# A two-layer mixer and expert kernel: three of the second scan's products dt\*x\*B move from VectorE to GpSimd

## The chip, the core and the metric

The kernel runs on one NeuronCore of a Trainium2 chip. Five engines work side by side and meet at semaphores: TensorE (PE in the profile; PEld is its weight load), VectorE (DVE), ScalarE (ACT), GpSimd (POOL) and SyncE (SP, which here only issues DMAs). Each engine runs its own instruction stream in order. Times are microseconds on the device, the whole kernel from start to end; the metric is the median of several executions.

## The reference, cut to what matters

The input x is [2, 128, 16, 16]: 2 batches of 256 tokens with 128 channels. Layer 0 is a selective state-space mixer (Mamba) followed by 8 experts (top 2), layer 1 a decaying sum over time followed by 16 experts (top 2). The part that the change touches is the mixer's scan, for 256 inner channels and 16 states:

```
dt = softplus(dt @ dt_proj_w.T + dt_proj_b);  A = -exp(A_log)
def step(h, inp):
    dt_t, B_t, C_t, x_t = inp
    dA = exp(dt_t[..., None] * A)
    h  = dA * h + (dt_t * x_t)[..., None] * B_t[:, None, :]
    y  = einsum('bdn,bn->bd', h, C_t)
y = scan(step); y = (y + xc * D) * silu(z); out = layernorm(clamp(y @ out_proj_w.T))
x = x + out;  x = x + experts(layernorm(x))      # layer 0, each token weighs 2 of 8 experts
```

## The kernel before, in words

Everything stays in SBUF. Channels lie on the 128 partitions; the 256 inner channels are two chunks (DC = 2), time (T = 256) is the free axis. The 16 states go in 8 pairs (PAIR = 2, NP = 8). With two batches that makes 16 pairs, numbered m = k + 8\*b; a tile of a pair holds 2 states x 2 chunks x 256 times = 1024 values in each partition. The work of pair m is:

- PE, `spread_b` (L990): transposes spread the two B rows over all partitions into the PSUM bank `b_ps` (one bank, one pair at a time).
- DVE, `inputs` (L695, instruction L702): the product dtx\*B into the PSUM tile `dbx[m % 2]`.
- ACT, `decays` (L508, L520): four exponentials make the decay factors in the SBUF tile `da[m % 4]`, up to four pairs ahead of the scan.
- DVE, `states` (L705, L712): one scan instruction along time, from `da` and `dbx` into the SBUF tile `hs[m % 2]`. It waits for `hc_done` of pair m-2, since `hs` has two buffers.
- POOL, `weigh` (L336, L343): the scan's states times the C rows, into `hc[m % 2]`. The C rows come by DMA from a small DRAM buffer, spread to all partitions, in three parts (`C_PARTS`).
- PE, `add` (L1000, L1004): matmuls with the identity sum the pair into PSUM.

All engines walk one list of steps, `plan` (L233 to L253), and each issues what it has in a step. For a pair the steps are `pair_in` and `pair_out`. DVE makes the product of pair m+1 in `pair_in` of pair m, and the scan of m in `pair_out`; POOL has nothing in `pair_in`, and `weigh` in `pair_out`. Between the pairs of the second batch (L241 to L247) the plan puts the tail of batch 0: its output projection, two norms, the routing and the first expert unit. The two lines that set this order are

```
before_states = {1: ["gate_out", "out_proj"], 3: ["inner_norm", "root_5"], 4: ["logits"], 5: ["softmax_e"], 7: ["lead"]}
after_states = {1: ["out_norm", "root_3"], 2: ["skip_norm", "skip_stats", "root_4"], 3: ["inner_scale", "to_channel"], ...}
```

The `root_` steps are inverse square roots on POOL (L310 to L313), for which DVE waits in the normalisation that follows: `skip_norm` needs `root_3`, `inner_norm` needs `root_4`. In steps `stage` (after `pair_in` of pairs k = 0 and 2) POOL makes the low parts of two expert weight blocks each (L357). `gates` and `softmax_e` (L785 to L813) route the tokens on DVE; the first `experts` unit needs the products of all 16 pairs done, since its PSUM banks are theirs, and the sum of pair 15 (`last_sum`) stands between units 1 and 2. After that PE works through 64 expert units (2 layers x 2 batches x 16).

Of the kernel before, what the change touches and what calls it, by code (L numbers as in the profile page):

```python
# [31 lines left out]
F32 = mybir.dt.float32  # L32
# [49 lines left out]
xt_ps var1 rstd1 var2 rstd2 xtok_ready taps_ps taps_ready wv_ps wv_ready xs_tok xs_ps xs_ready conv_ps xc_ready z_ps sz_ready  # L82
bct_ps bct_ready c_row_ready c_row_stored c0_loaded c1_loaded c2_loaded dt_ps abs_done r_done relu_done exp_dt ln_dt dt0_ready rounded dt1_ready dtx_ready
conv1_ps
# [8 lines left out]

def bass_metaformer(nc, x, packed, taps, rows, w1_0, w2_0, b2, decay, w1_1, w2_1, c_rows, out):
    with ExitStack() as ctx:
# [34 lines left out]
        b_tok = sb("b_tok", [128, NB, TT, NS])  # L130
        c_row = sb("c_row", [NS, NB, T])
        dt_a = per_batch("dt_a", [128, DC, T])
        dt_e = per_batch("dt_e", [128, DC, T])
        dt_l = per_batch("dt_l", [128, DC, T])
        dt_q = per_batch("dt_q", [128, DC, T])
# [87 lines left out]
        def between(work, end, groups, layer, b):  # L223
# [3 lines left out]
            for k in range(singles):  # L227
# [28 lines left out]
        @block.sync  # L256
        def _(sp):
            sp.dma_start(x_cm[:, 0, :], x[:, 0, :]).then_inc(s["x0_loaded"], 16)
            sp.dma_start(x_cm[:, 1, :], x[:, 1, :]).then_inc(s["x1_loaded"], 16)
            sp.dma_start(rows_sb[:], rows).then_inc(s["rows_loaded"], 16)  # L260
            sp.dma_start(par[:], packed).then_inc(s["params_loaded"], 16)
            sp.dma_start(cb[:, NP - DC:NP].rearrange("p c i t -> p (c i t)"), taps.to_broadcast([C, DC * TAPS * 128])).then_inc(s["taps_loaded"], 16)
            sp.dma_start(decay_sb[:], decay).then_inc(s["decay_loaded"], 16)
            sp.dma_start(b2_sb[:], b2).then_inc(s["b2_loaded"], 16)

            def weights(layer, i, w1_d, w2_d):
                n = EXPERTS[layer] // 2
# [9 lines left out]
            def c_rows_round(b):  # L277

                sp.wait_ge(s["c_row_ready"], b + 1)
                sp.dma_start(c_rows[b], c_row[:, b, :]).then_inc(s["c_row_stored"], 16)  # L280
                sp.wait_ge(s["c_row_stored"], 16 * (b + 1))
                for i, (k0, k1) in enumerate(C_PARTS):
                    if b:
                        sp.wait_ge(s["hc_done"], k1 + RING)
                    sp.dma_start(cb[:, k0:k1].rearrange("p k i t -> p (k i t)"),
                                 c_rows[b, PAIR * k0:PAIR * k1].rearrange("(o n) t -> o (n t)", o=1).to_broadcast([128, (k1 - k0) * PAIR * T])
                                 ).then_inc(s[f"c{i}_loaded"], 16)

            weights(0, 0, w1_0, w2_0)
            c_rows_round(0)  # L290
            weights(0, 1, w1_0, w2_0)
            for i in range(2):
                weights(1, i, w1_1, w2_1)
            c_rows_round(1)
# [7 lines left out]
        def _(pool):  # L302
# [88 lines left out]
            for step, *arg in plan:  # L391
# [7 lines left out]
                elif step == "root_5":  # L399
                    root_5(*arg)  # L400
                elif step == "step_1":
                    step_1()
                elif step == "step_x":
                    step_x()
                elif step == "stage":
                    low_part(0, arg[0], arg[0])
                elif step == "pair_out":
                    weigh(*arg, arg[1] % RING)
                elif step == "expert_in":
                    expert_in(*arg)  # L410
                elif step == "experts":
                    experts(*arg)
# [3 lines left out]
        def _(act):  # L416
# [91 lines left out]
            def decays(b, k, q):  # L508
# [3 lines left out]
                if b and k == 0:  # L512
                    act.wait_ge(s["dt1_ready"], 1)
                if m >= AHEAD:
                    act.wait_ge(s["h_done"], m + (1 + RING - AHEAD))
                for c in range(DC):
                    if b == 0 and k == 0:
                        act.wait_ge(s["dt0_ready"], c + 1)
                    for i in range(PAIR):
                        ins = nc.scalar.activation(da[q][:, i, c, 1:T], dt[:, c, b, 1:T], ACT.Exp,  # L520
                                                   scale=a_neg[:, c * NS + k * PAIR + i:c * NS + k * PAIR + i + 1])
# [73 lines left out]
        def _(dve):  # L595
# [99 lines left out]
            def inputs(b, k, p):  # L695
# [185 lines left out]
        def _(pe):  # L881
# [80 lines left out]
            def bc(b):  # L962
# [238 lines left out]
```

## Time and profile before

| | us |
|---|---|
| median of 3 runs | 215.6 (214.52 to 215.91) |
| the profiled execution | 212.92 |
| its span in the profile | 211.0 |
| busy in it: PE, PEld, DVE, ACT, POOL | 180.6, 149.6, 135.5, 120.1, 104.4 |

The span is the part of an execution that the profile shows. Lines such as L712 are lines of the kernel's file. A line of a timeline gives the start, the busy time, engine, line, operation, output and inputs, the shape, how many instructions are merged, and in brackets the idle time before it with what ended it. The instructions of one engine overlap by some 0.04 to 0.1 us, so the distance from start to start is what one of them costs in a queue.

### The profile page before, as it was taken

The numbers are of one execution on the slowest core, as the hardware profiler recorded it, in microseconds if no ns is written. First come the engines' busy times: TensorE is split into PE (matmuls) and PEld (weight loads), VectorE is DVE, ScalarE is ACT, GpSimd is POOL, SyncE is SP. The second block draws the span as 40 slices with busy tenths as digits, with TensorE's granted clock in tenths as the row PEclk, the third lists the DMA queues.
The fourth block names the chain that finished last, engine by engine and source line by source line (L and its number), as shares of the span: only waits on it lengthen the run. The fifth ranks groups of instructions, "written<-read, shape, count | busy, mean of one in ns | idle before, by whom it ended". The sixth has DMA issues, their size and how long they took to land. (4 is left out here: it accounts for less than half of the span.)

```text
span 211.0 us, 3706 instructions
## 1 busy us (share of the span) xinstructions
PE 180.6 (86%) x1194; PEld 149.6 (71%) x1194; DVE 135.5 (64%) x317; ACT 120.1 (57%) x276; POOL 104.4 (49%) x136
## 2 busy tenths in 40 slices
PE   6789677995887387499999999699998999999993
PEld 5467454542353243267999989699997999999992
DVE  2764689999899999972373846563158573433433
ACT  2717995999850039143578646567564655455540
POOL 5410034579796955475575435444456244444500
PEclk9999999999999979999999999999999999999998
DMA  6950199995540000000000000000000000000000
GB/s 182 307 153 0 59 393 341 324 321 165 199 165 37 2 0 0 0 0 0 3 2 0 3 2 0 3 0 0 3 2 0 3 0 5 0 26 3 0 0 25
DMA packets 7233, 14.38 MB, mean 68 GB/s; under 512 B 512, under 2 KB 3112, under 8 KB 6960
## 3 DMA queue, kind: packets, MB, share of 16 engines
q1 hardware_dynamic: 7216, 14.17, 20.8%
q8 instruction: 9, 0.15, 0.3%
q14 instruction: 8, 0.07, 0.1%
HBM read 13.88 MB, written 0.29 MB: 67 GB/s over the span
## 5 line engine op out<-in xcount | busy, mean ns | idle before, releaser
L343 POOL TENSOR_TENSOR hc<-hs,cb 128x1024 f32<-128x1024 f32 x16 | 37.7, 2356 | 32.6 <-DVE hs L712 32.6
L836 DVE SCALAR_TENSOR_TENSOR acc<-dbx_ps,comb,acc 128x128 f32<-128x128 f32 x96 | 29.1, 344 | 36.6 <-PE dbx_ps L1106 35.6
L1081 PE MATMUL bc_ps<-x_hi,w_hi 128*128 128x256 f32 x128 | 41.8, 326 | 0.0
L563 ACT ACTIVATE hid<-bc_ps,par 128x256 f32<-128x256 f32 x64 | 26.8, 469 | 24.9 <-PE bc_ps L1083 24.8
L357 POOL TENSOR_TENSOR w_lo<-w1b,w_hi 128x256 fp32r<-128x256 f32 x32 | 23.5, 735 | 27.6 <-ACT w_hi L555 27.3
L712 DVE TENSOR_TENSOR_SCAN hs<-da,dbx_ps 128x1024 f32<-128x1024 f32 x16 | 36.5, 2278 | 0.1
L1083 PE MATMUL bc_ps<-x_hi,w_lo 128*128 128x256 f32 x128 | 36.2, 283 | 0.0
L1082 PE MATMUL bc_ps<-x_lo,w_hi 128*128 128x256 f32 x128 | 36.0, 281 | 0.0
L1106 PE MATMUL dbx_ps<-w2a,hid 128*128 128x128 f32 x256 | 34.1, 276 | 0.5 <-issue 0.3
L1106 PE MATMUL dbx_ps<-w2b,hid 128*128 128x128 f32 (+1 forms) x256 | 33.9, 276 | 0.5 <-DVE acc L836 0.5
L357 POOL TENSOR_TENSOR w_lo<-w1a,w_hi 128x256 fp32r<-128x256 f32 x32 | 23.1, 729 | 21.6 <-ACT w_hi L555 21.6
L566 ACT ACTIVATE hid<-bc_ps 128x512 f32<-128x512 f32 x32 | 19.1, 597 | 24.1 <-PE bc_ps L1083 23.9
L1106 PEld LDWEIGHTS dbx_ps<-w2a,hid 128*128 128x128 f32 x256 | 31.4, 192 | 1.2 <-ACT hid L563 0.6
L1106 PEld LDWEIGHTS dbx_ps<-w2b,hid 128*128 128x128 f32 x256 | 31.3, 191 | 1.1 <-issue 0.7
L520 ACT ACTIVATE da<-dt,a_neg 128x255 f32<-128x255 f32 x64 | 26.5, 493 | 2.8 <-DVE hs L712 2.7
L1081 PEld LDWEIGHTS bc_ps<-x_hi,w_hi 128*128 128x128 f32 x128 | 24.4, 191 | 0.6 <-issue 0.5
L1082 PEld LDWEIGHTS bc_ps<-x_lo,w_hi 128*128 128x128 f32 x128 | 24.5, 191 | 0.5 <-issue 0.5
L1083 PEld LDWEIGHTS bc_ps<-x_hi,w_lo 128*128 128x128 f32 x128 | 24.3, 189 | 0.0
L996 PEld LDWEIGHTS bc_ps<-ident,b_tok 128*128 128x128 f32 x64 | 7.0, 141 | 21.7 <-DVE dbx_ps L702 16.9
L996 PE MATMUL bc_ps<-ident,b_tok 128*128 128x128 f32 x64 | 10.7, 292 | 13.1 <-DVE dbx_ps L702 11.5
L702 DVE TENSOR_TENSOR dbx_ps<-dtx,bc_ps 128x1024 f32<-128x1024 f32 x16 | 19.6, 1223 | 1.7 <-PE bc_ps L996 0.8
L1004 PE MATMUL y_ps<-hc,ident 128*128 128x512 f32 x32 | 16.7, 647 | 3.4 <-POOL hc L343 3.4
(164 smaller groups left out, 227.1 us busy)
## 6 DMA issues: line engine op xcount, KB each, us to landing
w1a<-w_in SPq DMA_DIRECT2D x2, 1024.0 KB, 9.0
cb<-c_rows SPq DMA_DIRECT2D x2, 1024.0 KB, 6.8
w1b<-w_in SPq DMA_DIRECT2D x2, 1024.0 KB, 13.7
cb<-c_rows SPq DMA_DIRECT2D x2, 768.0 KB, 5.2
cb<-taps_in SPq DMA_DIRECT2D x1, 512.0 KB, 5.2
cb<-c_rows SPq DMA_DIRECT2D x2, 256.0 KB, 3.8
par<-packed_in SPq DMA_DIRECT2D x1, 473.0 KB, 3.4
x_cm<-x_in SPq DMA_DIRECT2D x2, 128.0 KB, 2.2
```

The lines of the kernel that those rows point to most:

```text
L343: nc.gpsimd.tensor_tensor(hc[p][:], hs[p][:], cb[:, k].rearrange("p i (o t) -> p i o t", o=1).to_broadcast([128, PAIR, DC, T]), ALU.mult). ...
L357: nc.gpsimd.tensor_tensor(w1_lo[p][:], w1[layer][:, bass.ds(u * UW, UW)], w1_hi[p][:].bitcast(F32), ALU.subtract).then_inc(s["w1_staged"], 1)
L520: ins = nc.scalar.activation(da[q][:, i, c, 1:T], dt[:, c, b, 1:T], ACT.Exp, scale=a_neg[:, c * NS + k * PAIR + i:c * NS + k * PAIR + i + 1])
L563: ins = nc.scalar.activation(hid[p][:, c, :], h_ps[:, p, T * c:T * (c + 1)], ACT.Gelu, bias=par[:, bass.ds(u * UC + at, 1)])
L566: ins = nc.scalar.activation(hid[p][:], h_ps[:, p, :].rearrange("p (c t) -> p c t", c=UC), ACT.Gelu)
L702: nc.vector.tensor_tensor(dbx[p], dtx[b][:].rearrange("p (o c) t -> p o c t", o=1).to_broadcast([128, PAIR, DC, T]), rows.to_broadcast([12 ...
L712: nc.vector.tensor_tensor_scan(*flat, 0.0, ALU.mult, ALU.add).then_inc(s["h_done"], 1)
L836: nc.vector.scalar_tensor_tensor(acc[k][:, t, :], o_ps[:, w // span % RING, 128 * t:128 * (t + 1)], comb[layer][b][:, t, bass.ds(u, 1)], a ...
L1081: nc.tensor.matmul(h_ps[:, p, T * c:T * (c + 1)], w1_hi[w][:, at], x_hi[b][:], start=True, stop=False)
L1082: nc.tensor.matmul(h_ps[:, p, T * c:T * (c + 1)], w1_hi[w][:, at], x_lo[b][:], start=False, stop=False)
L1083: ins = nc.tensor.matmul(h_ps[:, p, T * c:T * (c + 1)], w1_lo[w][:, at], x_hi[b][:], start=False, stop=True)
L1106: ins = nc.tensor.matmul(o_ps[:, bank, 128 * t:128 * (t + 1)], hid[p][:, c, 128 * t:128 * (t + 1)], w2[layer][:, bass.ds(u * UC + c, 1), : ...
```

## The change

For pairs m = 10, 12 and 14 (of the second batch) the product dtx\*B is made by POOL, in a new function `product`, from B rows that a DMA has spread to all partitions in SBUF, into one SBUF tile `dbx_sb`. POOL issues it in `pair_in` of pair m-2. For these pairs the decay factors are written to the PSUM tile `dbx[m % 2]` that the product would have used, so the scan still has one input in SBUF and one in PSUM. DVE's product and PE's `spread_b` of these pairs fall away. The DRAM buffer carries the B and C rows, 32 in place of 16, and SP issues three more DMAs of 256 KB each after the first part of the C rows. To make room in SBUF, `dt_a`, `dt_e`, `dt_l` and `dt_q` have one buffer for both batches.

```diff
+ON_POOL = (NP + 2, NP + 4, NP + 6)
+B_SLOT = (0, 1, 2)
...
+        dbx_sb = sb("dbx_sb", [128, PAIR, DC, T])
+        b_wide = [sb(f"b_wide_{p}", [128, PAIR, T]) for p in range(2)] + [xs_b[:].rearrange("p (i t) c -> p i (t c)", i=PAIR)]
...
+        def made(m):
+            return m - sum(p < m for p in ON_POOL)
...
+                    if i == 0:
+                        for j, m in enumerate(ON_POOL):
+                            if m // NP == b:
+                                k = m % NP
+                                sp.dma_start(b_wide[B_SLOT[j]][:].rearrange("p i t -> p (i t)"),
+                                             bc_rows_d[b, PAIR * k:PAIR * (k + 1)].rearrange("(o n) t -> o (n t)", o=1).to_broadcast([128, PAIR * T])
+                                             ).then_inc(s["b_wide_loaded"], 16)
...
+            def product(m):
+                b, j = m // NP, ON_POOL.index(m)
+                pool.wait_ge(s["b_wide_loaded"], 16 * len(ON_POOL))
+                pool.wait_ge(s["dtx_ready"], 1)
+                if j:
+                    pool.wait_ge(s["h_done"], ON_POOL[j - 1] + (1 + RING))
+                nc.gpsimd.tensor_tensor(dbx_sb[:], dtx[b][:].rearrange("p (o c) t -> p o c t", o=1).to_broadcast([128, PAIR, DC, T]),
+                                        b_wide[B_SLOT[j]][:].rearrange("p i (o t) -> p i o t", o=1).to_broadcast([128, PAIR, DC, T]),
+                                        ALU.mult).then_inc(s["dbx_pool"], 1)
...
+                elif step == "pair_in":
+                    if arg[1] + NP * arg[0] + RING in ON_POOL:
+                        product(arg[1] + NP * arg[0] + RING)
...
-                if m >= AHEAD:
+                dst = da[q][:]
+                if m in ON_POOL:
+                    dst = dbx[m % RING]
+                    act.wait_ge(s["h_done"], m + 1)
+                    nc.scalar.activation(dst[:, :, :, 0:1], da[q][:, :, :, 0:1], ACT.Copy)
+                elif m >= AHEAD:
...
-                dve.wait_ge(s["dbx_done"], m + (1 + RING))
+                if m in ON_POOL:
+                    dve.wait_ge(s["dbx_pool"], ON_POOL.index(m) + 1)
...
-                if 1 < m < NB * NP:
+                if 1 < m < NB * NP and m not in ON_POOL:
                     inputs(m // NP, m % NP, m % RING)
...
-                if m < NB * NP:
+                if m < NB * NP and m not in ON_POOL:
                     spread_b(m // NP, m % NP)
```

## Rows read from the trace of the kernel before

**Rows 1.** Busy time by stage, from the second scan on (columns: stretch, length, engines, granted clock, DMA)

```profile
53.90:93.40 39.50, 27.71 (x106) 14.59 (x104) 38.59 (x52) 15.44 (x38) 27.61 (x24) 0.96 0.15 51
93.40:207.60 114.20, 110.51 (x918) 106.73 (x918) 55.73 (x205) 64.52 (x159) 52.70 (x77) 1.00 0.01 3
```

**Rows 2.** The chain that ended last, by engine, from the page

```profile
PE 33%; DVE 3%; issue 1%; POOL 1%; DVEq 0%; POOLq 0%
```

**Rows 3.** Timeline of DVE in the second scan

```profile
60.95 1.23 DVE L702 TENSOR_TENSOR dbx_ps<-dtx,bc_ps 128x1024 f32<-128x1024 f32 x1
62.09 0.68 DVE L728 TENSOR_TENSOR dtx<-m_ps,sz 128x512 f32<-128x512 f32 x1
62.69 2.28 DVE L712 TENSOR_TENSOR_SCAN hs<-da,dbx_ps 128x1024 f32<-128x1024 f32 x1
...
66.00 1.21 DVE L702 TENSOR_TENSOR dbx_ps<-dtx,bc_ps 128x1024 f32<-128x1024 f32 x1
67.12 2.27 DVE L712 TENSOR_TENSOR_SCAN hs<-da,dbx_ps 128x1024 f32<-128x1024 f32 x1
69.31 0.70 DVE L623 TENSOR_SCALAR m_ps<-norm_a,mv,rstd 128x128 f32<-128x128 f32 x2
...
71.65 1.21 DVE L702 TENSOR_TENSOR dbx_ps<-dtx,bc_ps 128x1024 f32<-128x1024 f32 x1
73.07 0.73 DVE L623 TENSOR_SCALAR m_ps<-t_tok,mv,rstd 128x128 f32<-128x128 f32 x2 [0.21 <-POOL rstd L313]
...
81.61 0.16 DVE L789 TENSOR_REDUCE zsum<-z_exp 128x2 f32<-128x16 f32 x1
...
82.01 0.73 DVE L791 TENSOR_TENSOR prob<-z_exp,zsum 128x16 f32<-128x16 f32 x1
82.78 2.29 DVE L712 TENSOR_TENSOR_SCAN hs<-da,dbx_ps 128x1024 f32<-128x1024 f32 x1
...
85.86 1.65 DVE L807 TENSOR_TENSOR comb<-prob,left 128x16 f32<-128x16 f32 x1
...
87.54 1.22 DVE L702 TENSOR_TENSOR dbx_ps<-dtx,bc_ps 128x1024 f32<-128x1024 f32 x1
```

**Rows 4.** Timeline of POOL in the second scan

```profile
59.75 1.40 POOL L357 TENSOR_TENSOR w_lo<-w1a,w_hi 128x256 fp32r<-128x256 f32 x2
61.11 2.36 POOL L343 TENSOR_TENSOR hc<-hs,cb 128x1024 f32<-128x1024 f32 x1
...
67.67 0.71 POOL L313 TENSOR_TENSOR rstd<-rstd,neg_half 128x2 f32<-128x2 f32 x1
68.34 1.41 POOL L357 TENSOR_TENSOR w_lo<-w1a,w_hi 128x256 fp32r<-128x256 f32 x2
69.70 2.35 POOL L343 TENSOR_TENSOR hc<-hs,cb 128x1024 f32<-128x1024 f32 x1
...
72.32 0.71 POOL L313 TENSOR_TENSOR rstd<-rstd,neg_half 128x2 f32<-128x2 f32 x1
...
80.35 2.36 POOL L343 TENSOR_TENSOR hc<-hs,cb 128x1024 f32<-128x1024 f32 x1 [1.80 <-DVE hs L712]
82.67 0.73 POOL L350 TENSOR_TENSOR x_lo<-x_full,x_hi 128x256 fp32r<-128x256 f32 x1
85.14 2.34 POOL L343 TENSOR_TENSOR hc<-hs,cb 128x1024 f32<-128x1024 f32 x1 [1.75 <-DVE hs L712]
```

**Rows 5.** Timeline of PE: the sum of pair 7, and of pair 14

```profile
59.84 1.98 PE L1004 MATMUL m_ps<-hc,ident 128*128 128x512 f32 x4 [0.46 <-POOL hc L343]
...
93.43 1.98 PE L1004 MATMUL y_ps<-hc,ident 128*128 128x512 f32 x4 [0.23 <-POOL hc L343]
```

**Rows 6.** SP's issue of the three DMAs of the second C rows

```profile
52.34 7.79 SPq L285 DMA_DIRECT2D cb<-c_rows  x3
```

**Rows 7.** DMA traffic behind it, windows (last two columns: DMA share, GB/s)

```profile
57.00:58.00 1.00, 1.00 (x3) 0.19 (x1) 0.91 (x2) 0.61 (x2) 0.57 (x1) 1.00 0.18 74
58.00:59.00 1.00, 0.53 (x4) 0.27 (x4) 1.00 (x2) 1.00 (x3) 1.00 (x1) 1.00 0.00 0
```

**Rows 8.** Timeline of ACT: the decay factors that waited for the scan of pair 8

```profile
60.90 1.70 ACT L520 ACTIVATE da<-dt,a_neg 128x255 f32<-128x255 f32 x4 [1.81 <-DVE hs L712]
```

More of the change, by code:

```diff
@@ L82 @@
 xt_ps var1 rstd1 var2 rstd2 xtok_ready taps_ps taps_ready wv_ps wv_ready xs_tok xs_ps xs_ready conv_ps xc_ready z_ps sz_ready
-bct_ps bct_ready c_row_ready c_row_stored c0_loaded c1_loaded c2_loaded dt_ps abs_done r_done relu_done exp_dt ln_dt dt0_ready rounded dt1_ready dtx_ready
+bct_ps bct_ready bc_row_ready bc_row_stored c0_loaded c1_loaded c2_loaded b_wide_loaded dbx_pool dt_ps abs_done r_done relu_done exp_dt ln_dt dt0_ready rounded dt1_ready dtx_ready
 conv1_ps
@@ L91, with bass_metaformer @@
 """.split()
-def bass_metaformer(nc, x, packed, taps, rows, w1_0, w2_0, b2, decay, w1_1, w2_1, c_rows, out):
+def bass_metaformer(nc, x, packed, taps, rows, w1_0, w2_0, b2, decay, w1_1, w2_1, bc_rows_d, out):
     with ExitStack() as ctx:
@@ L130, in bass_metaformer @@
         b_tok = sb("b_tok", [128, NB, TT, NS])
[L131 to L135, printed above, removed]
+        bc_row = sb("bc_row", [BC, NB, T])
+        dt_a = [sb("dt_a", [128, DC, T])] * NB
+        dt_e = [sb("dt_e", [128, DC, T])] * NB
+        dt_l = [sb("dt_l", [128, DC, T])] * NB
+        dt_q = [sb("dt_q", [128, DC, T])] * NB
         dt = sb("dt", [128, DC, NB, T])
@@ L275, in weights, with rows_round @@
                              ).then_inc(s[f"w2_{layer}_loaded"], 16)
[L277 to L281, printed above, removed]
+            def rows_round(b):
+                sp.wait_ge(s["bc_row_ready"], b + 1)
+                sp.dma_start(bc_rows_d[b], bc_row[:, b, :]).then_inc(s["bc_row_stored"], 16)
+                sp.wait_ge(s["bc_row_stored"], 16 * (b + 1))
                 for i, (k0, k1) in enumerate(C_PARTS):
@@ L285, in c_rows_round @@
                     sp.dma_start(cb[:, k0:k1].rearrange("p k i t -> p (k i t)"),
-                                 c_rows[b, PAIR * k0:PAIR * k1].rearrange("(o n) t -> o (n t)", o=1).to_broadcast([128, (k1 - k0) * PAIR * T])
+                                 bc_rows_d[b, NS + PAIR * k0:NS + PAIR * k1].rearrange("(o n) t -> o (n t)", o=1).to_broadcast([128, (k1 - k0) * PAIR * T])
                                  ).then_inc(s[f"c{i}_loaded"], 16)
+                    if i == 0:
[5 more added lines that the diff above has]
+                                             ).then_inc(s["b_wide_loaded"], 16)
             weights(0, 0, w1_0, w2_0)
-            c_rows_round(0)
+            rows_round(0)
             weights(0, 1, w1_0, w2_0)
@@ L293, in _ @@
                 weights(1, i, w1_1, w2_1)
-            c_rows_round(1)
+            rows_round(1)
             for b in range(NB):
@@ L490, in bc_copy @@
                 act.wait_ge(s["bct_ps"], b + 1)
-                nc.scalar.activation(c_row[:, b, :], bct_ps[b][0:NS, T:2 * T], ACT.Copy).then_inc(s["c_row_ready"], 1)
+                nc.scalar.activation(bc_row[:, b, :], bct_ps[b][0:BC, T:2 * T], ACT.Copy).then_inc(s["bc_row_ready"], 1)
                 nc.scalar.activation(b_tok[:, b], bct_ps[b][:, 0:TT * NS].rearrange("p (t r) -> p t r", t=TT),
@@ L519, in decays @@
                     for i in range(PAIR):
-                        ins = nc.scalar.activation(da[q][:, i, c, 1:T], dt[:, c, b, 1:T], ACT.Exp,
+                        ins = nc.scalar.activation(dst[:, i, c, 1:T], dt[:, c, b, 1:T], ACT.Exp,
                                                    scale=a_neg[:, c * NS + k * PAIR + i:c * NS + k * PAIR + i + 1])
@@ L699, in inputs @@
                 dve.wait_ge(s["h_done"], m + 1)
-                dve.wait_ge(s["b_ready"], m + 1)
+                dve.wait_ge(s["b_ready"], made(m) + 1)
                 rows = b_ps.rearrange("p (i o t) -> p i o t", i=PAIR, o=1)
@@ L706, in states @@
                 m = k + NP * b
-                dve.wait_ge(s["dbx_done"], m + (1 + RING))
+                if m in ON_POOL:
+                    dve.wait_ge(s["dbx_pool"], ON_POOL.index(m) + 1)
+                    src = dbx_sb[:].rearrange("p i c t -> p (i c t)")
+                else:
+                    dve.wait_ge(s["dbx_done"], made(m) + (1 + RING))
+                    src = dbx_ps[:, 2 * p:2 * p + 2, :].rearrange("p i t -> p (i t)")
                 dve.wait_ge(s["da_done"], m + 1)
                 dve.wait_ge(s["hc_done"], m + 1)
-                flat = (hs[p][:].rearrange("p i c t -> p (i c t)"), da[m % AHEAD][:].rearrange("p i c t -> p (i c t)"),
-                        dbx_ps[:, 2 * p:2 * p + 2, :].rearrange("p i t -> p (i t)"))
+                flat = (hs[p][:].rearrange("p i c t -> p (i c t)"), (dbx[p] if m in ON_POOL else da[m % AHEAD][:]).rearrange("p i c t -> p (i c t)"),
+                        src)
                 nc.vector.tensor_tensor_scan(*flat, 0.0, ALU.mult, ALU.add).then_inc(s["h_done"], 1)
@@ L974, in bc @@
                 for c in range(DC):
-                    ins = nc.tensor.matmul(bct_ps[b][0:NS, T:2 * T], w[:, c, DTR + NS:DTR + BC], xc[:, c, b, :],
+                    ins = nc.tensor.matmul(bct_ps[b][0:BC, T:2 * T], w[:, c, DTR:DTR + BC], xc[:, c, b, :],
                                            start=(c == 0), stop=(c == DC - 1))
@@ L990, in spread_b @@
             def spread_b(b, k):
-                pe.wait_ge(s["dbx_done"], k + (NP * b + RING))
+                pe.wait_ge(s["dbx_done"], made(k + NP * b) + RING)
                 for i in range(PAIR):
@@ L1089, in lead @@
                 pe.wait_ge(s["w2_0_loaded"], 32)
-                pe.wait_ge(s["dbx_done"], NB * NP + RING)
+                pe.wait_ge(s["dbx_done"], made(NB * NP) + RING)
                 pe.wait_ge(s["rounded"], 1)
@@ L1193 @@
           for name, a in arrays.items()}
-    c_rows = nc.dram_tensor("c_rows", (NB, NS, T), F32, kind="Internal").ap()
+    bc_rows = nc.dram_tensor("bc_rows", (NB, BC, T), F32, kind="Internal").ap()
     y = nc.dram_tensor("y_out", (NB, C, T), F32, kind="ExternalOutput").ap()
@@ L1197 @@
                     ap["w1_0_in"], ap["w2_0_in"], ap["b2_in"], ap["decay_in"],
-                    ap["w1_1_in"], ap["w2_1_in"], c_rows, y.rearrange("b c t -> c b t"))
+                    ap["w1_1_in"], ap["w2_1_in"], bc_rows, y.rearrange("b c t -> c b t"))
     r = run_bass_kernel_spmd(nc, [arrays], core_ids=[0])
```

## The prediction, made before the changed kernel was run

> **What bounds the kernel now.** I first cut the span into stages by the busy times of windows [rows 1]. From 93.4 us on PE is busy for 110.5 of 114.2 us at the full granted clock of 1.00 (2.4 GHz): the stream of expert units, which the change doesn't touch. The chain of waits says the same: it is mostly PE, and reaches back only into the experts [rows 2]. So the change acts through one number, the time at which that stream begins. PE's last wait for the scan stage is the sum of pair 14, which starts at 93.43, when POOL's weighing ends [rows 5]. Before that, from 53.9 to 93.4, DVE is busy for 38.6 of 39.5 us, POOL for 27.6 and PE for 27.7 [rows 1]: DVE bounds the stage by its sum. By that alone, three products fewer are a gain. Their price is the distance from a product to what follows: 62.09 - 60.95 = 1.14 and 67.12 - 66.00 = 1.12 [rows 3], three of them 3.4 us.
>
> But in DVE's timeline one wait stands out: before the normalisation L623 at 73.07 DVE idles for 0.21 us, until POOL's inverse root (L313, 72.32 + 0.71 = 73.03) is there [rows 3, 4]. POOL is then already as late as DVE. The second thing to see is that two tiny DVE instructions with both inputs in SBUF, L791 and L807 on 16 values, take 0.73 and 1.65 us, and end at 82.74 and 87.51, each 0.03 us after POOL's weighing has ended (80.35 + 2.36 = 82.71; 85.14 + 2.34 = 87.48) [rows 3, 4]. They are held until POOL's instruction is through. DVE's products and scans, with one input in PSUM, aren't held: the scan at 62.69 ran beside the weighing at 61.11 and took 2.28 us [rows 3, 4]. The Trainium skill says this in "SBUF — State Buffer", Who interferes with whom: a VectorE instruction with two SBUF inputs shares a read port with a GpSimd instruction that reads SBUF, and the later one is blocked for the whole of the other. The trace agrees.
>
> **The change part by part.** I walk the two queues through the change, with durations of the same trace. A POOL product reads and writes as much as a weighing, 128x1024 from SBUF with one input repeated, so it is priced as one: 2.32 us from start to start (80.35 to 82.67) [rows 4]. No nearer row exists; I keep 2.2 to 2.6.
>
> *First product, pair 10.* POOL issues it after weighing pair 7, in the place where L357 begins, at 59.75 [rows 4]; it needs its B rows by then. Of the C rows, the first two parts (1 MB) are issued from 52.34 on, and the traffic has ended by 58 us [rows 6, 7]. After the change the first megabyte in the queue is the first C part and the three B blocks, so they land at about 57.5 to 58.5, a cover of over 1 us. The second C part follows, in time for pair 9. POOL's queue becomes: product 59.75, two low parts 62.07, weighing of pair 8 at 62.07 + 1.36 = 63.43 (1.36 is 59.75 to 61.11), of pair 9 at 65.75. From the start of a weighing to the end of the inverse root behind it are 73.03 - 69.70 = 3.33 us [rows 4], so `root_3` ends at 69.08 (before: 67.67 + 0.71 = 68.38).
> DVE is 1.14 us free at 60.9, but its next step, L728, reads the sum of pair 7, and PE's matmuls for that end at 59.84 + 1.98 = 61.82 [rows 5]. It starts at 61.86 in place of 62.09: 0.23 of the 1.14 us come in. Then scan 9 at 62.46 (+0.60), product 11 at 65.77 (+3.31), scan 10 at 66.89 (+1.12), `skip_norm` at 69.08 (+2.19), all distances from [rows 3]. Scan 10 also waits for weighing 8, done at 65.8, and its decays, below: neither is late. `skip_norm` needs `root_3`, at 69.08: just in time. The first product is worth 0.2 us at this point.
>
> *Second product, pair 12.* This is where it decides. POOL issues it ahead of `stage`, weighing 10 and `root_4`, and it waits for scan 10, since there is one `dbx_sb`. Scan 10 ends at 66.89 + 2.27 = 69.16; POOL starts 0.07 us behind a scan (82.78 + 2.29 to 85.14), so at 69.23. The low parts follow at 71.55, weighing 10 at 72.91, and `root_4` ends at 72.91 + 3.33 = 76.24. DVE has finished `skip_norm` and its statistics at 69.08 + (71.65 - 69.31) = 71.42, has no product to make, and waits nearly 5 us for `inner_norm`, which starts at 76.28 instead of 73.07: **+3.21 us**. Behind that wait in DVE's order stand scan 11 and all that comes after. In words: before, the low parts could begin at 68.34, while DVE still scanned; now they stand behind a product that begins 0.89 us later and takes 2.32.
>
> *Third product, pair 14.* POOL starts it behind scan 12, at 80.35 + 3.21 = 83.56, in the place of weighing 12. DVE, without its own product, would reach L791 at most 1.13 us sooner than 82.01 + 3.21 = 85.22, so not before 84.1. Either way POOL's product holds it until 83.56 + 2.36 = 85.92, and it ends at 85.95 = 82.74 + 3.21. Nothing comes in. Now POOL goes on: weighing 12 at 85.88, x_lo (L350) at 88.20, and weighing 13, for which scan 13 (85.99 to 88.28) is done, at 88.88 (0.68 for a low part, half of 1.36). DVE reaches L807 at 85.99 + (85.86 - 82.78) = 89.07, behind weighing 13 by 0.19 us, and is held until 88.88 + 2.34 + 0.03 = 91.25. Before it was free at 87.51: +3.74, so **another 0.53 us**.
>
> *Edits with no price.* The decays of pairs 10, 12 and 14 may run one scan ahead where they ran three ahead. Those of pair 10 start when scan 8 is done, at 60.90, and take 1.70 us [rows 8], plus a copy of 4 values, at most another 0.43: done by 63.1, wanted at 66.89. Pair 12's start at 69.2 and are wanted at 81, pair 14's at 84 and wanted at 92. Behind the wait in ACT's queue stand two weight roundings, which POOL reads at 71.5. Scans with the two memories swapped I price as before, 2.28. The three DMA issues come before the third C part, which waits for weighing 7 anyway [rows 6]. The 32 rows in place of 16 and the transposes saved on PE lie beside longer work. PE idles longer between the sums, and its mean granted clock in this stage is already 0.96 [rows 1]; a sum at 1.2 GHz would come some 1 us later, but `root_4`, L791 and L807 are what end last. I keep 0 to 0.4 us.
>
> *The rest moves along.* Product 15, scans 14 and 15, the weighings and the sum of pair 14 keep their distances to L807, so PE's stream begins 3.74 us later. Sum: 3.21 + 0.53 = 3.74 us. Span 211.0 + 3.7 = 214.7, execution 212.92 + 3.7 = 216.7; the profiled execution lies 2.7 us below the median, so against that: 215.6 + 3.7 = **219.3 us**, 1.7% slower.
>
> The Trainium skill warns against such a move in "Perfetto Trace Analysis", Optimizing Scalar/DVE Operations: the two engines share an SBUF read port, so shifting work between them may not help. Here only L791 and L807 show it. If that were all, and POOL's order cost nothing, the walk above would leave a gain: 0.23 and 1.12 us from the first two products, nothing from the third, less the 0.53 us of L807, some 0.8 us.
>
> **The rivals.**
>
> *A, not slower by what can be told: L807 slips in ahead of weighing 13.* My margin is only 0.19 us. If POOL is 0.2 us later or DVE 0.2 sooner, the two small instructions take about 0.20 us each (as 81.61 to 82.01) in place of 1.68 (87.54 - 85.86), product 15 starts at 89.47 in place of 87.54, and the total is +1.9: 217.5 us, 0.9%. For it: the margin. Against: both sides start from the same event, the end of POOL's product. The Trainium skill's rule in the same section of "SBUF — State Buffer", that order of issue decides who is blocked, is this case. Chance 0.15.
>
> *B: L791 isn't let in between two POOL instructions.* Before, x_lo follows weighing 12 at once (82.67), and L791 still ends at 82.74, which speaks against it [rows 3, 4]. If it had to wait for weighing 12 too, it would end at 88.27, scan 13 would run to 90.6, weighing 13 to 93.0, and L807 end at 93.0: +5.5, 221.1 us. Chance 0.1.
>
> *C: the B rows land late.* Every microsecond beyond 59.8 comes on top, less 0.15. If the four transfers moved at half the rate of before (5.7 us from 52.34 to 58, so 11.3), POOL would start at 63.7: some +7, 223 us. A smaller delay is likelier; I give 0.06 at about 221.
>
> *D: faster.* All of the 3.4 us would come in if POOL had its roots ready in time, 212.2 us at best. For that `root_4` would have to end at 71.4 instead of 76.2; even a product of no length leaves it at 73.9. The rows exclude it as long as POOL keeps the plan's order. Chance 0.04.
>
> **How the numbers follow.** Forecast 0.62 (with product lengths of 2.2 to 2.6, which count once or twice, and the clock's 0.4: 3.4 to 4.6 us, so 219.0 to 220.2), A 0.15 at 217.0 to 217.8, B 0.1, C 0.06, D 0.04, others 0.03. The range takes in A and most of B: 217.0 to 221.2. Some 1% (2.2 us) is what a measurement of this kernel can tell from no change, its three runs spread over 0.65%. Slower by over 1%: forecast, B, C and a share of the others, 0.80. Within 1%: most of A, 0.15. Faster: 0.05.
>
> **What the profile after would show.** DVE idle for 4 to 5 us before L623 at about 76.3, put down to POOL's L313. The gain at L728 only 0.2 us. POOL products of 2.3 us at 59.8, 69.2 and 83.6. L791 held for about 1.5 us, L807 for about 2.2. PE's stream of experts from 97.2 on, unchanged in length. I would be wrong if POOL's product were much shorter or longer than a weighing, if the B rows were late, or if the roots didn't stand where I read them in the plan.

## The result, and the profile after

The changed kernel takes 219.19 us (median of 4 runs, 218.5 to 219.66) against 215.19 for the kernel before (4 runs, 214.52 to 215.91): 4.0 us or 1.8% slower, ratio 1.0183 with a 95% interval of 1.0135 to 1.023. The forecast was 219.3, slower by 3.7. Some executions are over 1.5% slower than the fastest of their kernel; the ratios below leave them out, the medians don't.

The profiled executions differ by more, spans of 217.9 and 211.0 us. Of these 6.9 us, 1.4 had come in before the second scan (the scan of pair 7 starts at 56.50 instead of 55.07; TensorE's convolution matmuls took 6.41 instead of 5.26 us) and 1.5 in the experts, where the granted clock of one stretch was 0.57. Executions of one kernel differ by more than these two parts together: in the later comparisons the kernel before alone lay between 212.8 and 217.2 us. So the traces are compared below over one stretch, **S**: from the start of the scan of pair 7 to the start of TensorE's sum of pair 14, from which on the expert stream is dense. Before: 93.43 - 55.07 = 38.36 us. After: 98.82 - 56.50 = 42.32, **3.96 us longer**. That is the size of the 4.0 us between the medians.

VectorE after the change, timeline. The rows answer to [rows 3]; L657 is L623 there, L751 is L712, L767 L728, L830 L791 and L846 L807:

```profile
60.01 2.28 DVE L751 TENSOR_TENSOR_SCAN hs<-da,dbx_ps 128x1024 f32<-128x1024 f32 x1
63.28 0.69 DVE L767 TENSOR_TENSOR dtx<-m_ps,sz 128x512 f32<-128x512 f32 x1 [1.00 <-PE m_ps L1043]
...
68.32 2.28 DVE L751 TENSOR_TENSOR_SCAN hs<-dbx_ps,dbx_sb 128x1024 f32<-128x1024 f32 x1
70.97 0.72 DVE L657 TENSOR_SCALAR m_ps<-norm_a,mv,rstd 128x128 f32<-128x128 f32 x2 [0.38 <-POOL rstd L328]
...
73.17 0.25 DVE L648 BATCH_NORM_AGGREGATE mv<-stats 128x2 f32<-128x6 f32 x2
77.86 0.73 DVE L657 TENSOR_SCALAR m_ps<-t_tok,mv,rstd 128x128 f32<-128x128 f32 x2 [4.44 <-POOL rstd L328]
78.63 2.29 DVE L751 TENSOR_TENSOR_SCAN hs<-da,dbx_ps 128x1024 f32<-128x1024 f32 x1
...
86.03 1.59 DVE L830 TENSOR_TENSOR prob<-z_exp,zsum 128x16 f32<-128x16 f32 x1
87.65 2.29 DVE L751 TENSOR_TENSOR_SCAN hs<-da,dbx_ps 128x1024 f32<-128x1024 f32 x1
...
90.74 2.16 DVE L846 TENSOR_TENSOR comb<-prob,left 128x16 f32<-128x16 f32 x1
```

Three products are gone, and where the second stood VectorE now sits idle for 4.44 us. What it waits for is in GpSimd's timeline, the answer to [rows 4]:

```profile
61.56 2.35 POOL L369 TENSOR_TENSOR dbx_sb<-dtx,b_wide 128x1024 f32<-128x1024 f32 x1 [0.36 <-DMA xs_b<-bc_rows]
63.87 1.42 POOL L383 TENSOR_TENSOR w_lo<-w1a,w_hi 128x256 fp32r<-128x256 f32 x2
65.24 4.64 POOL L358 TENSOR_TENSOR hc<-hs,cb 128x1024 f32<-128x1024 f32 x2
...
70.16 0.71 POOL L328 TENSOR_TENSOR rstd<-rstd,neg_half 128x2 f32<-128x2 f32 x1
70.83 2.35 POOL L369 TENSOR_TENSOR dbx_sb<-dtx,b_wide 128x1024 f32<-128x1024 f32 x1
73.13 1.42 POOL L383 TENSOR_TENSOR w_lo<-w1a,w_hi 128x256 fp32r<-128x256 f32 x2
74.49 2.35 POOL L358 TENSOR_TENSOR hc<-hs,cb 128x1024 f32<-128x1024 f32 x1
...
77.12 0.71 POOL L328 TENSOR_TENSOR rstd<-rstd,neg_half 128x2 f32<-128x2 f32 x1
...
85.24 2.35 POOL L369 TENSOR_TENSOR dbx_sb<-dtx,xs_b 128x1024 f32<-128x1024 f32 x1 [1.90 <-DVE hs L751]
87.55 2.34 POOL L358 TENSOR_TENSOR hc<-hs,cb 128x1024 f32<-128x1024 f32 x1
89.85 0.72 POOL L376 TENSOR_TENSOR x_lo<-x_full,x_hi 128x256 fp32r<-128x256 f32 x1
90.53 2.34 POOL L358 TENSOR_TENSOR hc<-hs,cb 128x1024 f32<-128x1024 f32 x1
```

Read it down: from 61.56 to 77.83 GpSimd has no gap above 0.1 us, and the inverse root that VectorE's normalisation needs comes last, behind a product (70.83), two low parts and a weighing. TensorE, the answer to [rows 5], and the windows of the stage, the answer to [rows 1] (columns as there):

```profile
92.92 1.99 PE L1043 MATMUL y_ps<-hc,ident 128*128 128x512 f32 x4 [1.00 <-POOL hc L358]
94.74 0.38 PE L1103 MATMUL m_ps<-ident,comb 128*8 128x128 f32 x2
...
98.82 1.98 PE L1043 MATMUL y_ps<-hc,ident 128*128 128x512 f32 x4 [0.23 <-POOL hc L358]
```

```profile
53.90:97.10 43.20, 31.77 (x86) 15.60 (x87) 36.02 (x49) 16.18 (x42) 34.16 (x27) 0.76 0.19 67
97.10:214.00 116.90, 113.48 (x930) 109.40 (x928) 57.04 (x203) 65.58 (x162) 54.39 (x78) 0.99 0.01 2
```

VectorE's busy time in the stage fell from 38.59 to 36.02 us, GpSimd's rose from 27.61 to 34.16, and the stage grew. Relieving the busiest engine made the stage longer.

Two chains lead from GpSimd's weighing of pair 13 to the sum of pair 14, and they are almost equally long. One runs through VectorE: L846 is held to the end of that weighing (92.90), then product 15, scan 14 and weighing 14 follow, and the sum starts 5.92 us behind L846's end. The other runs through TensorE: the sum of pair 13 (92.92) waits for the same weighing, and the transposes of the gates (94.74), the first expert unit and its bias stand behind it; TensorE is through with them some 0.2 us sooner than weighing 14, by the wait of 0.23 us before 98.82. In the kernel before it was the same, 5.92 us from L807's end and a wait of 0.23 us [rows 3, 5], with these rows of TensorE ahead:

```profile
87.54 1.98 PE L1004 MATMUL y_ps<-hc,ident 128*128 128x512 f32 x4 [2.79 <-POOL hc L343]
89.36 0.38 PE L1064 MATMUL m_ps<-ident,comb 128*8 128x128 f32 x2
```

### The profile page after: what moved, and what is told of

The parts are those of the page before. It is cut to its first block and busy times, and to the rows that moved or that the text cites. A ratio compares the mean times of both kernels' runs of the same rounds, so it can differ in the third digit from the quotient of the medians.

```text
span 217.9 us, 3688 instructions
## 1 busy us (share of the span) xinstructions
PE 187.6 (86%) x1182; PEld 153.6 (70%) x1182; DVE 133.5 (61%) x314; ACT 120.5 (55%) x279; POOL 111.2 (51%) x139
## 5 line engine op out<-in xcount | busy, mean ns | idle before, releaser
L1145 PE MATMUL dbx_ps<-w2a,hid 128*128 128x128 f32 x256 | 35.0, 281 | 0.5 <-issue 0.3
L1145 PEld LDWEIGHTS dbx_ps<-w2a,hid 128*128 128x128 f32 x256 | 32.2, 196 | 1.2 <-ACT hid L597 0.6
L751 DVE TENSOR_TENSOR_SCAN hs<-da,dbx_ps 128x1024 f32<-128x1024 f32 x13 | 29.6, 2280 | 0.1
L1043 PE MATMUL y_ps<-hc,ident 128*128 128x512 f32 x32 | 20.8, 791 | 8.2 <-POOL hc L358 8.2
L554 ACT ACTIVATE da<-dt,a_neg 128x255 f32<-128x255 f32 x52 | 21.6, 493 | 0.1
L1043 PE MATMUL m_ps<-hc,ident 128*128 128x512 f32 x32 | 16.7, 649 | 2.5 <-POOL hc L358 2.5
L1043 PEld LDWEIGHTS y_ps<-hc,ident 128*128 128x128 f32 x32 | 7.1, 242 | 16.6 <-POOL hc L358 11.1
L736 DVE TENSOR_TENSOR dbx_ps<-dtx,bc_ps 128x1024 f32<-128x1024 f32 x13 | 15.9, 1224 | 1.6 <-PE bc_ps L1035 0.8
```

The costliest lines, as they stand in the source:

```text
L554: ins = nc.scalar.activation(dst[:, i, c, 1:T], dt[:, c, b, 1:T], ACT.Exp, scale=a_neg[:, c * NS + k * PAIR + i:c * NS + k * PAIR + i + 1])
L1043: ins = nc.tensor.matmul(y_bank[b], ident[:], hc[p][:, i], start=False, stop=(last and i == PAIR - 1))
L1145: ins = nc.tensor.matmul(o_ps[:, bank, 128 * t:128 * (t + 1)], hid[p][:, c, 128 * t:128 * (t + 1)], w2[layer][:, bass.ds(u * UC + c, 1), : ...
```

## The experiments

Eleven kernels ran, in three comparisons. In each the kernel before ran on the same chip, with medians of 215.01, 215.26 and 214.96 us. S is worked out from each kernel's own trace, as start of the sum of pair 14 less start of the scan of pair 7.

| kernel | S, us | against S before | median, us | before beside it | ratio (95%) |
|---|---|---|---|---|---|
| before | 93.43 - 55.07 = 38.36 | | 215.19 | | |
| after | 98.82 - 56.50 = 42.32 | +3.96 | 219.19 | 215.19 | 1.0183 (1.0135 to 1.023) |
| e1, product 12 behind root_5 | 96.56 - 56.92 = 39.64 | +1.28 | 217.51 | 215.01 | 1.0134 (1.005 to 1.0219) |
| e2, products 10 and 14 only | 94.89 - 55.40 = 39.49 | +1.13 | 217.14 | 215.01 | 1.0116 (1.0031 to 1.02) |
| e3, after + router in PSUM | 99.61 - 57.05 = 42.56 | +4.20 | 218.98 | 215.01 | 1.019 (1.0096 to 1.0285) |
| e4, before + router in PSUM | 94.53 - 57.02 = 37.51 | -0.85 | 213.97 | 215.01 | 0.9983 (0.9935 to 1.003) |
| e5, after + scan 11 before the norm | 98.76 - 56.66 = 42.10 | +3.74 | 218.31 | 215.26 | 1.0183 (1.0093 to 1.0273) |
| e6, e4 + TensorE order | 93.94 - 57.25 = 36.69 | -1.67 | 214.91 | 215.26 | 0.9871 (0.982 to 0.9923) |
| e7, two products, all mended | 92.88 - 56.46 = 36.42 | -1.94 | 212.6 | 215.26 | 0.9882 (0.9803 to 0.9961) |
| e8, after + extra matmuls | 99.35 - 57.08 = 42.27 | +3.91 | 219.18 | 215.26 | 1.0201 (1.0106 to 1.0296) |
| e9, e3 + TensorE order | 96.47 - 56.28 = 40.19 | +1.83 | 216.92 | 214.96 | none |
| e10, three products, all mended | 92.17 - 55.54 = 36.63 | -1.73 | 212.3 | 214.96 | 0.9886 (0.9842 to 0.993) |
| e11, no product, all mended | 93.28 - 56.86 = 36.42 | -1.94 | 214.07 | 214.96 | 0.9864 (0.9799 to 0.993) |

The medians carry the scatter of whole executions, some 2 us; S leaves out what lies outside the stage. S comes from one trace of each kernel. How well such a time repeats can be read where the order of VectorE and GpSimd is the same: the second normalisation starts 21.36, 21.29, 21.31 and 21.30 us behind scan 7 in the changed kernel, e3, e8 and e9, and 18.00, 17.99 and 17.99 us in the kernel before, e4 and e6. The changed kernel itself has no runs in these three comparisons. So a kernel is set against it by S; by whole times e1 and e2 can't be told from it, since their intervals overlap with 1.0135 to 1.023. e9 has no ratio; its four runs lie from 214.75 to 218.83 us.

**e1: the same work in another order.** GpSimd makes product 12 behind `root_5`.

```diff
                 elif step == "root_5":
                     root_5(*arg)
+                    if arg[-1] == 0:
+                        product(NP + 4)
...
-                    if arg[1] + NP * arg[0] + RING in ON_POOL:
+                    if arg[1] + NP * arg[0] + RING in ON_POOL and arg[1] != 2:
```

> The changed kernel with one move: GpSimd makes the product of pair 12 after root_4 and root_5, no longer before stage, weighing 10 and root_4. Same work. Theory (the order in GpSimd's queue costs, because root_4 stands behind product 12): root_4 is some 2.5 us earlier, VectorE's wait before inner_norm falls from 4.4 to under 2 us, and the whole is 2.2 to 2.9 us faster than the changed kernel: about 216.5. Rival (a product on GpSimd costs wherever it stands, since GpSimd holds the port against VectorE): within 1 us of the changed kernel, 218.2 to 219.2.

S is 2.68 us shorter than that of the changed kernel, as the theory had it; nothing but a place in a queue was changed. The median came down by less, to 217.51 (216.5 expected). In its timeline the root is no longer behind the product, and VectorE's wait is halved:

```profile
75.61 0.73 DVE L659 TENSOR_SCALAR m_ps<-t_tok,mv,rstd 128x128 f32<-128x128 f32 x2 [2.14 <-POOL rstd L328]
```

**e2: pair 12 given back to VectorE.** `ON_POOL = (NP + 2, NP + 6)`.

> The changed kernel with pair 12 given back to VectorE, pairs 10 and 14 still on GpSimd. Theory: the wait for root_4 shrinks from 4.4 us to about 1, VectorE does 1.1 us more, product 14 now runs before scan 12 has ended and pushes weighing 12 so that L791 and L807's counterparts are held about 1.2 us more than before the change: in all 2.2 to 2.9 us faster than the changed kernel, about 216.5. Rival (each product on GpSimd costs its third of the loss): 1.3 us faster, 217.9.

S is 2.83 us shorter than after: one of three products holds most of the loss, not a third of it. The other two still leave +1.13 us, where I had written 1.2.

**e3 and e4: the small router instructions are no longer held.** In `softmax_e` the inverse sum, and in `gates` the values left after the top two, stand in PSUM (in a free part of `m_ps`), for batch 0 of layer 0, in the changed kernel (e3) and in the one before (e4).

```diff
-                link(nc.vector.reciprocal(zsum[b][:], zsum[b][:]))
+                z_inv = m_ps[:, T + 128:T + 128 + TT]
+                link(nc.vector.reciprocal(z_inv, zsum[b][:]))
...
                 pr, rest_p = prob[layer][b], left[layer][b]
+                if (layer, b) == (0, 0):
+                    rest_p = m_ps[:, T + 64:T + 64 + TT * (n + 8)].rearrange("p (t e) -> p t e", t=TT)
```

> The changed kernel, but the two small router instructions that GpSimd holds (in softmax_e and gates, batch 0 of layer 0) get one of their inputs in PSUM: the inverse sum, and the values left after the top two. Theory: they take 0.2 us each in place of 1.59 and 2.16, so some 3.4 us faster than the changed kernel, 215.8, while the 4.4 us wait for root_4 stays. Rival (the hold is the whole loss): after this the changed kernel beats the kernel before with the same edit by about 3 us.

> The kernel before, with the same two router inputs in PSUM, no product on GpSimd. Theory: 0.73 and 1.65 us become 0.2 each, 2.0 us faster than the kernel before, about 213.2, and 2.0 to 3.0 us faster than the changed kernel with this edit (the wait for root_4 remains there). Rival (the hold is the whole loss): the changed kernel with this edit would be the faster of the two.

The hold goes, as the rows of e3 show: 0.17 us each in place of 1.59 and 2.16, beside GpSimd instructions of 2.35 us. The lost time does not: S is 42.56, even 0.24 longer. Theory and rival both fell here. Why is in the rows behind it, VectorE first and then GpSimd and TensorE of e3:

```profile
86.52 0.17 DVE L831 TENSOR_TENSOR prob<-z_exp,m_ps 128x16 f32<-128x16 f32 x1
...
89.82 0.17 DVE L849 TENSOR_TENSOR comb<-prob,m_ps 128x16 f32<-128x16 f32 x1
...
96.27 0.41 DVE L859 COPY combT<-m_ps 8x256 f32<-8x256 f32 x1 [2.85 <-PE m_ps L1106]
```

```profile
91.01 2.34 POOL L358 TENSOR_TENSOR hc<-hs,cb 128x1024 f32<-128x1024 f32 x1
```

```profile
90.42 5.59 PE L1046 MATMUL y_ps<-hc,ident 128*128 128x512 f32 x8 [2.45 <-POOL hc L358]
95.85 0.38 PE L1106 MATMUL m_ps<-ident,comb 128*8 128x128 f32 x2
```

GpSimd's weighing of pair 13 ends at 93.35, which is 36.30 us behind scan 7; in the changed kernel it is 92.87 - 56.50 = 36.37. Its queue is what it was. TensorE has the sum of pair 13 ahead of the gate transposes (L1106) and the experts' first hidden layer, so all of these wait for that weighing, with or without the hold. And TensorE, idle for 2.45 us before the two sums, falls to half clock in them: its granted clock is 1.00 up to 91, 0.64 from 91 to 92 and 0.50 from 92 to 94. The transposes start 2.50 us behind the end of weighing 13, where in the changed kernel, at a granted clock of 1.00, they start 1.87 us behind it. So the 0.24 us comes from the clock; at full clock, by estimate from these rows, e3 would have been 0.4 us shorter than the changed kernel, and no more.

In e4 the same edit brings 0.85 us of the 2.0 expected, since there too the sum of pair 13 has to wait for its weighing; the ratio, 0.9983, doesn't tell it from the kernel before. With this edit on both sides the products cost 5.05 us of S (42.56 against 37.51), where 2.0 to 3.0 were expected.

**e5: fill the wait with a scan.** `inner_norm` goes behind the scan of pair 11, from `before_states[3]` to the head of `after_states[3]`.

> The changed kernel with VectorE's inner_norm moved behind the scan of pair 11, so that VectorE scans while it would wait for root_4; GpSimd's queue is untouched. Theory (VectorE's wait for root_4 carries the loss): the scan fills 2.2 of the 4.4 us, root_5 and inner_scale then end last, the second scan is 1.3 us shorter, about 217.9 us. Rival (GpSimd's own chain up to the weighing of pair 13 carries it, VectorE only follows): weighing 13 ends no sooner than before and the kernel stays at 219.2.

VectorE did as expected: its wait fell to 2.57 us and scan 15 began 0.99 us sooner against scan 7 (39.08 to 40.07). Weighing 13 also ended 1.3 us sooner (91.73 - 56.66 = 35.07 against 36.37), so the rival is wrong. But S gained only 0.22 of the 1.3 expected. TensorE idled for 4.18 us, and the sums of pairs 12 and 13, ahead of the transposes, then ran at a granted clock of 0.50 (88.8 to 94.0), so that the transposes start 3.25 us behind the end of weighing 13:

```profile
88.80 6.34 PE L1043 MATMUL y_ps<-hc,ident 128*128 128x512 f32 x8 [4.18 <-POOL hc L358]
94.98 0.38 PE L1103 MATMUL m_ps<-ident,comb 128*8 128x128 f32 x2
```

**e6: TensorE's order, without products on GpSimd.** The sum of pair 13 moves behind the hidden layers of units 0 and 1.

```diff
-                elif k:
+                elif k and (b, k) != (1, NP - 2):
                     add(b, k - 1, (k - 1) % RING)
...
                     if (k, u0, u1) == (0, 0, 1):
+                        add(1, NP - 3, (NP - 3) % RING)
                         pe.wait_ge(s["h_done"], NB * NP - 1 + RING)
```

> The kernel before with the router inputs in PSUM (as in e4) and one step of TensorE moved: the sum of pair 13 is issued behind the hidden layers of expert units 0 and 1 instead of ahead of the gate transposes. Theory (after the router edit TensorE's order ends last: the sum of pair 13 waits for weighing 13, and transposes and hidden layers stand behind it): unit 0 begins some 2 us sooner, the sum of pair 14 some 1.2 us sooner than in e4, 212.8 us. Rival (nothing but the scans counts): as e4, 214.0.

The first expert unit begins 31.85 us behind scan 7, in e4 33.88; S is 0.82 us shorter than in e4 (1.2 expected). The median of 12 runs, 214.91, shows nothing of it (212.8 expected), since the runs lie from 211.2 to 215.7; the ratio to the kernel before, 0.9871, does.

**e7, e10, e11: what are the products worth once nothing stands behind them?** All three have the router inputs in PSUM, TensorE's order of e6 and `inner_norm` behind scan 11. e7 has products 10 and 12 on GpSimd, e10 all three (product 12 behind `root_5` in both), e11 none.

> All that the runs point to, with products 10 and 12 on GpSimd (14 back on VectorE), product 12 behind root_5, inner_norm behind the scan of pair 11, router inputs in PSUM and TensorE's order as in e6. Theory: two products off VectorE are now worth 0.9 us over e6, 211.9 us, the fastest. Rival (GpSimd's queue is full in this stage, any product there costs as much as it saves): as e6 or up to 1 us slower.

> As e7, with all three products on GpSimd. Theory: VectorE is 1.1 us shorter again, TensorE follows weighing 13 and the sum of pair 14 is 0.6 us sooner than in e7: about 212.0 us. Rival (GpSimd is full there): 1 us or more slower than e7.

> As e7, with no product on GpSimd: the kernel before with the router inputs in PSUM, TensorE's order of e6 and inner_norm behind the scan of pair 11. It says what the products are worth once nothing stands behind them. Theory from the traces of e6 and e7: the second scan within 0.5 us of that of e7, the time about the same, 212 to 213 us. Rival (VectorE is the bound, products off it count in full): 2.3 us longer than e7's second scan.

S is 36.42, 36.63 and 36.42 us, the ratios 0.9882, 0.9886 and 0.9864 with intervals that overlap. The medians of e10 and e11, 212.3 and 214.07, say no more: their runs lie from 211.5 to 216.1 and from 211.0 to 215.6. These versions beat both kernels, the one before by about 1.2%, as e6 alone does; in these orders the products on GpSimd add nothing. Of the 0.9 us expected from e7 over e6, S shows 0.27; the 0.6 us expected from e10 over e7 wasn't there.

Where the saved products went can be read in the traces. The program lets the first expert unit begin only when VectorE has made the product of pair 15. In e7 and e11 the unit starts 0.21 and 0.24 us behind that product's end, and S hangs on VectorE. In e7 VectorE is 1.2 us ahead of e11 at the second normalisation (18.67 against 19.88 us behind scan 7), but then waits for GpSimd twice, for `root_5` and for product 12, and scan 12 starts no sooner (22.63 and 22.61). VectorE and then TensorE of e7:

```profile
76.84 0.61 DVE L792 TENSOR_SCALAR xg_tok<-m_ps,rstd_b 128x128 f32<-128x128 f32 x2 [0.99 <-POOL rstd_b L328]
...
79.09 2.29 DVE L753 TENSOR_TENSOR_SCAN hs<-dbx_ps,dbx_sb 128x1024 f32<-128x1024 f32 x1 [0.17 <-POOL dbx_sb L369]
...
86.62 1.22 DVE L738 TENSOR_TENSOR dbx_ps<-dtx,bc_ps 128x1024 f32<-128x1024 f32 x1
```

```profile
88.05 0.36 PE L1125 MATMUL bc_ps<-x_hi,w_hi 128*128 128x256 f32 x1
```

In e10 VectorE stays ahead (scan 15 starts 33.04 us behind scan 7, in e11 33.77), but GpSimd makes product 14 before it weighs pair 12. TensorE's sum of pair 12 waits for that weighing, and the transposes and the first unit follow it without a gap. GpSimd and TensorE of e10:

```profile
80.65 2.35 POOL L369 TENSOR_TENSOR dbx_sb<-dtx,xs_b 128x1024 f32<-128x1024 f32 x1 [0.18 <-DVE hs L753]
82.96 2.35 POOL L358 TENSOR_TENSOR hc<-hs,cb 128x1024 f32<-128x1024 f32 x1
```

```profile
85.36 1.98 PE L1048 MATMUL y_ps<-hc,ident 128*128 128x512 f32 x4 [0.83 <-POOL hc L358]
87.18 0.38 PE L1108 MATMUL m_ps<-ident,comb 128*8 128x128 f32 x2
```

**e8: is it TensorE's clock?** Five extra matmuls into a free bank ahead of each of four sums; their results aren't used.

```diff
             def pair_out(b, k):
+                if b and 2 <= k <= 5:
+                    for _ in range(5):
+                        nc.tensor.matmul(f_ps[:, 0:T], ident[:], ones[:], start=True, stop=True)
```

> The changed kernel with five extra matmuls (ident by ones, into a bank that is free in this stage) ahead of each of the sums of pairs 9 to 12 in the second scan, so that TensorE is busier and its granted clock, 0.5 to 0.8 there in the changed kernel, is nearer to 1.00. Theory: root_4 and weighing 13 end last, not TensorE, so at most 0.5 us faster than the changed kernel: 218.7 to 219.2. Rival (the loss is TensorE's lower clock): 2 us or more faster, 217 or less.

Windows of the changed kernel, then of e8 (the third number from the end is the granted clock):

```profile
75.00:85.00 10.00, 6.33 (x11) 2.82 (x12) 7.10 (x9) 2.44 (x6) 6.41 (x8) 0.53 0.00 0
85.00:95.00 10.00, 7.69 (x19) 3.24 (x18) 9.48 (x18) 4.91 (x12) 7.63 (x4) 0.79 0.00 0
```

```profile
75.00:85.00 10.00, 5.30 (x21) 3.11 (x20) 6.58 (x8) 2.17 (x6) 6.94 (x9) 0.97 0.00 0
85.00:95.00 10.00, 10.00 (x32) 6.52 (x32) 9.48 (x18) 5.19 (x13) 7.63 (x4) 0.85 0.00 0
```

The clock in the middle of the stage rose from 0.53 to 0.97, S stayed (42.27 to 42.32), the median too (219.18). So the lower clock isn't the cause of the loss in the changed kernel.

**e9: both edits in the changed kernel.** The router edit of e3 and TensorE's order of e6.

> The changed kernel with the router inputs in PSUM (e3) and TensorE's order of e6 (the sum of pair 13 behind the hidden layers of units 0 and 1). GpSimd's queue and VectorE's wait for root_4 are untouched. Theory (in e3 the weighing of pair 13 ended last through TensorE's order, so that edit brought nothing): gate transposes and hidden layers no longer stand behind weighing 13, the sum of pair 14 comes some 3.4 us sooner than in e3 and in the changed kernel, about 215.8 us. Rival (weighing 13 itself is what the rest needs): as e3, 219.0.

S is 2.37 us shorter than in e3, so the order was what blocked there. It isn't the 3.4 expected (and the median is 216.92, not 215.8), because the path now runs through the weighing before, that of pair 12:

```profile
89.67 1.98 PE L1046 MATMUL y_ps<-hc,ident 128*128 128x512 f32 x4 [1.32 <-POOL hc L358]
91.49 0.38 PE L1106 MATMUL m_ps<-ident,comb 128*8 128x128 f32 x2
...
93.13 1.88 PE L1046 MATMUL y_ps<-hc,ident 128*128 128x512 f32 x4
```

The sum of pair 12 waits 1.32 us for weighing 12, which stands behind product 14 in GpSimd's queue; transposes, hidden layers and the sum of pair 13 (93.13) follow without a gap, and the sum of pair 14 comes 3.34 us after that (96.47). Weighing 13 no longer holds anything. Against e6, the same edits without products, e9's S is 3.50 us longer.

## Why the prediction was right, point by point

- *First product, 0.23 us at L728.* Measured from scan 7: 63.28 - 56.50 = 6.78 against 62.09 - 55.07 = 7.02 [rows 3], 0.24 us. VectorE waits 1.00 us there for the sum of pair 7, so most of the saved product is lost at once.
- *B rows in time, with over 1 us of cover.* Wrong in this execution. The last block lands 5.9 us after its issue at 55.57, so 7.2 us behind the first issue (54.23), where the prediction had 6.2 at most. GpSimd waits 0.36 us for it, `root_3` comes late and VectorE waits 0.38 us for that. This was rival C, at a small price: in e3, e8 and e9, with the same transfers, GpSimd doesn't wait at all, and the second normalisation comes only 0.05 to 0.07 us sooner.
- *Length of a product.* 2.35 us, 2.31 from start to start (61.56 to 63.87), as a weighing; priced 2.32.
- *Second product, +3.21 us.* The normalisation starts 21.36 us behind scan 7, before 18.00 [rows 3]: +3.36. The late B rows are 0.07 of the 0.15 more; in e3, without them, it is +3.29, where product 12 starts 0.17 us behind the end of scan 10 (68.87 + 2.28 to 71.32) and the walk had 0.07. e1 shows that it is the place in GpSimd's queue: 2.7 us go with it, and with product 12 as a whole 2.8 (e2).
- *Third product, nothing gained at L791, and 0.53 more at L807.* L830 ends at 87.62, 31.12 behind scan 7 (before 27.67: +3.45), L846 at 92.90, 36.40 behind (before 32.44: +3.96). So 0.51 us more, as walked. The hold is there as named, and in the trace its chain ends last, by the 0.23 us above. What the prediction left out is TensorE's chain beside it: the sum of pair 13 waits for the same weighing 13, which has moved back in GpSimd's queue by as much. So the hold isn't what makes the end late: e3 takes it away and the end stays. The size came out right because L807's release and that sum hang on one instruction. The sentence "`root_4`, L791 and L807 are what end last" should have read "`root_4` and weighing 13".
- *TensorE's clock, 0 to 0.4 us.* e8: nothing in this kernel. The clock fell further than the prediction took it, from 0.96 to 0.76 over the stage, and a sum at half clock costs 1.8 us (76.90, 3.78 against 1.98), not some 1 us; but these sums aren't on the path. In e3 and e5, where the low clock reaches the sum of pair 13, the transposes come 0.6 and 1.4 us later behind weighing 13 than in the changed kernel.
- *Rivals.* A (L807 slips in ahead of weighing 13) didn't come: weighing 13 started at 90.53, L846 at 90.74, 0.21 us apart against 0.19 forecast. It would not have brought the total down to the +1.9 us at which it was priced, since e3, where the hold is gone altogether, is no faster. B: L830 was let in between two GpSimd instructions, ending at 87.62 with the next one started at 87.55. D: nothing for it.
- *The sum.* 3.74 forecast, 3.96 in the trace, 4.0 in the medians.

The Trainium skill says in "SBUF — State Buffer", Who interferes with whom, that a VectorE instruction with at most one input in SBUF, outside its 2-port modes, doesn't contend with GpSimd. e3 agrees: with one of the two inputs in PSUM the same instructions take 0.17 us beside GpSimd. Its advice in "Perfetto Trace Analysis", Optimizing Scalar/DVE Operations, that moving work between these two engines might not help, was right here, though the port that it names wasn't what most of the loss hung on: 2.7 of the 4.0 us go with the place of one product in GpSimd's queue (e1), and taking the holds away saved nothing (e3).

What stays open: e1 still has 1.28 us over the kernel before, and no run splits it between the third product and the rest. And no run puts product 14 behind weighing 12, so what the products would be worth then isn't shown.

## What to carry to other kernels

Before work is moved to an engine with idle time, walk its queue through the stage and ask which small result, such as an inverse root, is issued behind the new work and who waits for it; the idle share says nothing of that. An instruction that is held until another ends may hang on the same event as the real path; taking the hold away tells which. And when the relieved engine isn't followed by anything that can start sooner, the saved time isn't worth the move: here two or three products off VectorE were worth nothing even in the best order that was tried. Walk the new queue once more after each mending, too: with the root set free, product 14 ahead of weighing 12 was the next thing that TensorE waited for (e10).

## What the runs showed of the hardware that I had not expected

- TensorE at half clock beside waits: after an idle time of 4.18 us the granted clock was 0.50 for over 5 us of work, and two sums took 6.34 us (e5), where two took 3.60 in e8, whose extra matmuls had kept it busy. With 5 extra matmuls ahead of each of four sums the granted clock from 75 to 85 us was 0.97, without them 0.53.
- Four DMAs of 256 KB, each spread from two rows to all partitions, with one of 768 KB issued right behind them: the last of the four landed 7.2 us after the first issue in the changed kernel and 6.5 to 6.9 us after it in e1, e3, e5, e8, e9 and e10. Before the change one of 256 KB and one of 768 KB had left the queue by 58 us, 5.7 us after issue [rows 6, 7].
- The held VectorE instruction is let in between two GpSimd instructions that follow each other without a gap: L830 ends at 87.62, GpSimd's next one starts at 87.55.
